# Exponentials in two runs of three, ternary magnitudes one iteration earlier, and GpSimd work in pieces, in a two-layer decoder on one NeuronCore

## What is computed

```python
x = x + L0_attn(ln(x))    # 16 heads of 16, RoPE, causal softmax, fp32 accuracy
x = x + L0_xattn(ln(x))   # fp8 quantised product with the context
x = x + L0_ffn(ln(x))     # mixture of 16 experts (top 4 of 2 groups) + shared expert
x = x + L1_attn(ln(x))    # ternary weights, int8 activations, causal softmax
x = x + L1_xattn(ln(x))   # 4 experts chosen by token id: silu(h W) * (h W), W^T
x = x + L1_ffn(ln(x))     # ternary gate/up/down with an inner RMS norm
```

## Time and profile before

| | |
|---|---|
| median of 3 runs | 726.19 us (725.18 to 727.3) |
| the profiled execution | 725.6 us, span 723.7 us |
| mean granted TensorE clock | 0.879 |
| PE busy | 527.7 us, 73% |
| DVE busy | 471.7 us, 65% |
| ACT busy | 343.7 us, 47% |
| POOL busy | 135.4 us, 19% |
| chain that ended last | PE 42%, DVE 32%, ACT 14%, issue 8% |

### The profile page before, as it was taken

The page is one execution under the profiler, slowest core; times in us unless marked ns, Lnnn a source line. Parts: engine busy times, 40 slices in busy tenths (PEclk is TensorE's granted clock), DMA queues, the critical chain, the costliest instruction groups (busy, mean ns, idle before and its releaser), DMA issues.

```text
span 723.7 us, 11688 instructions
## 1 busy us (share of the span) xinstructions
PE 527.7 (73%) x4689; PEld 362.9 (50%) x4716; DVE 471.7 (65%) x1049; ACT 343.7 (47%) x543; POOL 135.4 (19%) x142
## 2 busy tenths in 40 slices
PE   2663728527998789997789978999867677465775
PEld 1331414315676567675566756676645445233443
DVE  3667796796568864588645855458544664456985
ACT  2332416514772257822678226772478439213454
POOL 2225245350000400000040000004000040002543
PEclk9776768867999999999999999999989989769679
DMA  6032122201000010000000000001000000000000
GB/s 202 1 137 91 47 67 85 83 39 59 2 1 1 3 58 1 2 1 1 1 25 36 1 1 1 1 2 59 5 25 1 2 1 1 0 1 0 1 29 30
DMA packets 5706, 20.01 MB, mean 28 GB/s; under 512 B 879, under 2 KB 3055, under 8 KB 5012
## 3 DMA queue, kind: packets, MB, share of 16 engines
q1 hardware_dynamic: 5652, 19.26, 7.9%
HBM read 18.21 MB, written 1.05 MB: 27 GB/s over the span
## 4 chain that ended last, share of the span: by engine, by line
PE 42%; DVE 32%; ACT 14%; issue 8%; POOL 1%; DMA 1%; SPq 0%; ACTq 0%; DVEq 0%; POOLq 0%
PE ps L842 14%; PE ps L870 9%; ACT L1230 4%; DVE nmx L1555 4%; PE ps L627 4%; DVE hs L1670 3%; PE ps L737 2%; ACT hs L1230 2%; DVE hs L1664 2%; DVE y L1452 2%; PE ps L852 2%; PE ps L649 1%; PE ps L609 1%; DVE hl L1675 1%; ACT hh L1237 1%
## 5 line engine op out<-in xcount | busy, mean ns | idle before, releaser
L1237 ACT ACTIVATE hh<-hs 128x512 f16<-128x512 f32 (+1 forms) x68 | 42.0, 618 | 129.0 <-DVE hs L1670 129.0
L1664 DVE TENSOR_TENSOR hs<-hs,ps 128x512 f32<-128x512 f32 (+1 forms) x68 | 45.6, 670 | 81.0 <-ACT hs L1230 49.5
L487 POOL TENSOR_TENSOR ve<-mv,half 128x2 f32<-128x2 f32 x24 | 5.4, 224 | 344.7 <-DVE mv L1445 344.7
L1675 DVE TENSOR_TENSOR hl<-hs,hh 128x512 f16<-128x512 f32 (+1 forms) x68 | 49.3, 726 | 28.6 <-ACT hh L1237 28.0
L1555 DVE TENSOR_REDUCE nmx<-ps 128x2 f32<-128x512 f32 (+1 forms) x96 | 61.0, 680 | 3.8 <-PE ps L682 3.6
L870 PE MATMUL ps<-w2h,hh 128*128 128x256 f16 x200 | 55.8, 279 | 1.4 <-DVE hl L1675 1.3
L870 PE MATMUL ps<-w2l,hh 128*128 128x256 f16 x200 | 55.2, 276 | 0.0
L870 PE MATMUL ps<-w2h,hl 128*128 128x256 f16 x200 | 55.1, 276 | 0.0
L1230 ACT ACTIVATE hs<-ps 128x512 f32<-128x512 f32 (+1 forms) x68 | 39.6, 582 | 23.6 <-PE ps L842 23.2
L1670 DVE TENSOR_TENSOR hs<-hs,ps 128x512 f32<-128x512 f32 (+1 forms) x68 | 45.2, 665 | 1.1
L1230 ACT ACT_TABLE_LOAD x35 | 44.9, 1283 | 0.6
(11 more groups left out here) (245 smaller groups left out, 1352.3 us busy)
## 6 DMA issues: line engine op xcount, KB each, us to landing
stage<-in_w SPq DMA_DIRECT2D x12, 800.0 KB, 4.2
tstage<-in_tern SPq DMA_DIRECT2D x4, 1024.0 KB, 4.9
cs<-in_ctxT SPq DMA_DIRECT2D x1, 1024.0 KB, 10.1
out_x<-xs SPq DMA_DIRECT2D x4, 256.0 KB, 2.2
w0s<-in_w SPq DMA_DIRECT2D x1, 768.0 KB, 7.1
xs<-in_x SPq DMA_DIRECT2D x1, 768.0 KB, 8.4
lnwb<-in_lnw SPq DMA_DIRECT2D x1, 512.0 KB, 3.7
xs<-in_x SPq DMA_DIRECT2D x1, 256.0 KB, 2.7
```

Source lines behind the costliest of these rows:

```text
L1237: act.activation(hh[:, n % 2, 0:w], hs[:, n % 2, 0:w], ACT.Copy).then_inc(e_hi.sem, 1)
L1664: TT(hs[:, n % 2, 0:w], hs[:, n % 2, 0:w], ps[:, up_bank(n), 0:w], ALU.mult).then_inc(e_hb.sem, 1)
L1675: TT(hl[:, n % 2, 0:w], hs[:, n % 2, 0:w], hh[:, n % 2, 0:w], ALU.subtract).then_inc(e_lo.sem, 1)
```

## The change

Four edits:

1. In the mixed iterations ACT does E0, E1, E2 in a run, then the Silus of pairs 0 to 2, then E3, E4, E5 in a run, then the Silus of pairs 3 and on. PE's and DVE's lists are rewritten to match, also for iterations 0 and 1, which have no pairs. `phase_a` now holds pairs 0 to 5 and the second phase begins with pair 6.
2. `magnitudes(2)` and `magnitudes(3)` move from `phase_a` of iterations 5 and 6 to late in iterations 4 and 5.
3. POOL's `split_lo` becomes four instructions of 400 columns instead of one of 1600; its product with the norm weight in the last feed-forward becomes two of 256 instead of one of 512.
4. In iteration 0, `context_scaled` on DVE stands ahead of `queries_keys(1, 0)` and not behind it, and `context_rounded(2)` behind both `low_parts`.

```diff
+LOW_PIECE = 400
...
             def split_lo(b, n):
                 g.wait_ge(wst_hi.sem, wst_hi.at(b, n + 1))
-                g.tensor_tensor(wl[n][:, b * W_SLICE:(b + 1) * W_SLICE], stage[:, n, :],
-                                wh[n][:, b * W_SLICE:(b + 1) * W_SLICE], ALU.subtract).then_inc(wst_lo.sem, 1)
+                for a in range(0, W_SLICE, LOW_PIECE):
+                    cols = slice(b * W_SLICE + a, b * W_SLICE + a + LOW_PIECE)
+                    last = g.tensor_tensor(wl[n][:, cols], stage[:, n, a:a + LOW_PIECE], wh[n][:, cols], ALU.subtract)
+                last.then_inc(wst_lo.sem, 1)
...
-                    g.tensor_tensor(fw[:, j, c * 512:(c + 1) * 512], fh[:, j, c * 512:(c + 1) * 512],
-                                    lnwb[:, c * 512:(c + 1) * 512], ALU.mult).then_inc(f_w.sem, 1)
+                    for a in (512 * c, 512 * c + 256):
+                        last = g.tensor_tensor(fw[:, j, a:a + 256], fh[:, j, a:a + 256], lnwb[:, a:a + 256], ALU.mult)
+                    last.then_inc(f_w.sem, 1)
```

PE's `phase_a`, first half, before and after (`-` and `+`):

```diff
                 ups(it, 0)
                 scores_exp(it, 1)
-                outs(it, 0)
+                if it + 1 >= B:
+                    first_turn(it + 1)
+                scores_exp(it, 2)
                 if it + 1 < B:
                     project(it + 1, 0)
+                if routes:
+                    router_norm_turned(it - 1)
+                scores_exp(it, 3)
+                outs(it, 0)
                 gates(it, 1)
                 if it + 1 >= B:
-                    first_turn(it + 1)
-                if routes:
-                    router_norm_turned(it - 1)
+                    project(it + 1, 0)
                 ups(it, 1)
-                scores_exp(it, 2)
-                outs(it, 1)
-                if it + 1 >= B:
-                    project(it + 1, 0)
-                gates(it, 2)
                 if routes:
                     logits(it - 1)
                 values(it, 0)
+                outs(it, 1)
+                gates(it, 2)
+                values(it, 1)
                 ups(it, 2)
-                scores_exp(it, 3)
                 outs(it, 2)
-                values(it, 1)
+                back(it, 0)
+                project(it + 1, 1)
                 gates(it, 3)
                 ups(it, 3)
-                back(it, 0)
-                project(it + 1, 1)
                 scores_exp(it, 4)
-                outs(it, 3)
-                gates(it, 4)
                 scores_exp(it, 5)
-                ups(it, 4)
-                outs(it, 4)
                 values(it, 2)
-                gates(it, 5)
                 if it + 1 < ITS:
                     stack(it + 1, 0)
                     stack(it + 1, 1)
-                ups(it, 5)
+                outs(it, 3)
+                gates(it, 4)
```

DVE's `phase_a`, first part:

```diff
-                hb(it, 0)
                 if it + 1 < B:
                     first_low(it + 1)
                 elif it + 1 < ITS:
                     first_norm(it + 1)
                 if routes:
                     normalised("router", it - 1, yr, False)
-                hc(it, 0)
+                if it == 0:
+                    context_scaled()
                 if it + 1 < B:
                     queries_keys(it + 1, 0)
-                if it == 0:
-                    context_scaled()
-                low(it, 0)
-                hb(it, 1)
+                hb(it, 0)
                 if routes:
                     experts_lo("moe", it - 1, 0)
-                hc(it, 1)
+                hc(it, 0)
+                if it + 1 >= B:
+                    queries_keys(it + 1, 0)
+                low(it, 0)
```

ACT's `phase_b1`, where the magnitudes go:

```diff
+                sil(it, 9)
+                if it + 1 < ITS:
                     maxima_turned(it + 1)
+                experts_hi("hash", b, 7)
+                high(it, 9)
+                if b < 2:
+                    magnitudes(b + 2)
                 sil(it, 10)
```

More of the change, by code:

```diff
@@ L940, in phase_a, with phase_b0 @@
                     stack(it + 1, 3)
+                ups(it, 4)
+                values(it, 3)
+                outs(it, 4)
+                scores_max(it + 1, 0)
+                gates(it, 5)
+                back(it, 1)
+                ups(it, 5)
+                scores_max(it + 1, 1)
                 outs(it, 5)
-                values(it, 3)
-                scores_max(it + 1, 0)
+            def phase_b0(it):
                 gates(it, 6)
-                back(it, 1)
+                turn32(o, o_ok.sem, o_ok.at(it, 2))
                 ups(it, 6)
-                scores_max(it + 1, 1)
+                scores_max(it + 1, 2)
                 outs(it, 6)
[L950 to L956, removed]
                 pe.wait_ge(f_lo.sem, f_turn["output", it] + 1)
@@ L963, in phase_b0 @@
                 mm.then_inc(att_ok.sem, 1)
+                gates(it, 7)
+                scores_max(it + 1, 3)
+                ups(it, 7)
+                outs(it, 7)
                 gates(it, 8)
-                scores_max(it + 1, 3)
+                turn16(qq, q_ok, it + 1)
                 ups(it, 8)
+                scores_max(it + 1, 4)
                 outs(it, 8)
[L968 to L971, removed]
                 if it == 0:
@@ L979, in phase_b0 @@
                 mm.then_inc(xa_ok.sem, 1)
+                gates(it, 9)
+                scores_max(it + 1, 5)
+                ups(it, 9)
                 outs(it, 9)
-                scores_max(it + 1, 5)
                 if it:
@@ L998, in phase_b1 @@
                 b = it - B
-                gates(it, 7)
[L1000 to L1005, removed]
+                gates(it, 6)
+                scores_max(it + 1, 2)
+                ups(it, 6)
+                turn16(qq, q_ok, it + 1)
+                outs(it, 6)
+                scores_max(it + 1, 3)
+                gates(it, 7)
                 pe.wait_ge(q_ev.sem, q_turn["output", b] + 1)
@@ L1011, in phase_b1 @@
                 mm.then_inc(att_ok.sem, 1)
+                ups(it, 7)
+                scores_max(it + 1, 4)
+                outs(it, 7)
+                gates(it, 8)
+                scores_max(it + 1, 5)
                 ups(it, 8)
-                scores_max(it + 1, 4)
                 outs(it, 8)
[L1015 to L1018, removed]
                 if b == 0:
                     router_turned(it)
+                gates(it, 9)
                 if it + 1 < ITS:
                     maxima_turned(it + 1)
+                ups(it, 9)
+                turn32(yr, y_ok.sem, ln_turn["tail", b] + 1)
+                outs(it, 9)
                 gates(it, 10)
                 ups(it, 10)
-                turn32(yr, y_ok.sem, ln_turn["tail", b] + 1)
                 outs(it, 10)
@@ L1253, in phase_a @@
                 exponentials(it, 1)
-                high(it, 0)
                 if it + 1 >= B:
                     first_turn(it + 1)
+                exponentials(it, 2)
+                sil(it, 0)
                 if routes:
@@ L1269, in phase_a @@
                 exponentials(it, 3)
-                high(it, 2)
                 stacks(it + 1, 0)
@@ L1324, in phase_b1 @@
                 b = it - B
+                sil(it, 6)
+                quantised("output", b)
+                high(it, 6)
                 sil(it, 7)
-                quantised("output", b)
                 high(it, 7)
@@ L1329, in phase_b1 @@
                 high(it, 8)
-                sil(it, 9)
-                high(it, 9)
                 if b == 0:
@@ L1791, in phase_b0 @@
                 moments_of("context", b)
-                low(it, 7)
+                low(it, 6)
                 maximum(it + 1, 3)
+                hb(it, 7)
                 normalised("context", b)
@@ L1812, in phase_b0 @@
                 link(last)
+                hc(it, 8)
+                low(it, 8)
                 if b:
@@ L1829, in phase_b0 @@
                 dve.wait_ge(x_ok.sem, 2 * b + 2)
+                hb(it, 10)
                 hc(it, 10)
@@ L1836, in phase_b1 @@
                 int8(o, [(scal[:, :], 1)])
-                hb(it, 7)
+                hb(it, 6)
                 maximum(it + 1, 2)
-                hc(it, 7)
-                low(it, 7)
+                hc(it, 6)
+                low(it, 6)
                 maximum(it + 1, 3)
```

113 lines of the change are left out of this document (54 added, 59 removed).

## The result

The changed kernel takes 751.55 us (median of 4 runs, 749.01 to 755.99), the kernel before 726.75 us: ratio 1.0348, 95% interval 1.0299 to 1.0396, so it is slower. The profiled execution took 749.0 us, its span is 747.1 us.

What follows compares the result with a forecast made beforehand. PE paces the mixed iterations, DVE ends iteration 0. Mixed +12.9, iteration 6 -0.5, iteration 7 +4.0, iterations 0 and 1 -11, feed-forward -1.2 sum to +4.2 on 726.2: 730.4 us; own range 724 to 740, with most of the faster rival 713 to 740.

Steps and rivals of the forecast that it cites:

- the wait for `vt`: Iteration 5, sign of being right: PE waits 2 to 3.5 us for the copied values.
- the start of iteration 1: Sign of being right: iteration 1's first Exp starts at about 100 us instead of 109.
- Table loads: ACT, whole kernel: 46 loads fewer take 59 us off ACT; at most what PE or DVE waits for comes back.
- The walk: Iteration 5, new lists timed item by item with row durations: +4.3 us, PE's work unchanged; iteration 3 alike: +3.6.
- the slower rival: Slower, as forecast, chance 0.52; its clock case: five iterations each lose 1.5 us more behind new waits, 738 us.
- For iterations 2 and 4 I take +2.5: Mixed iterations 2 and 4: +2.5 us each, an old stall at the second phase's end being partly filled.
- Iterations 0 and 1: Early context_scaled and shorter waits for POOL's pieces: -9 and -2 us, sum -11, bounds -5 and -15.
- Iteration 6: Walk gives 66.2 after against 66.7 before: -0.5 us; magnitudes leave, but the Exp runs hold pairs 0 and 3 back.
- Iteration 7: No other work there; Silu 3 comes behind E5 and the int8 output is turned later: +4.0 us.
- Feed-forward: Last feed-forward: halves of POOL's product save about 0.4 us of `y` in each of three places: -1.2 us.
- the loads were the pace: Faster rival, chance 0.32: mixed iterations win 1 us each, 707 us, or 716 with half; needs copied-values wait under 1 us.
- The halves cancel: Rival, chance 0.16: mixed iterations lose 2 us each, iterations 0 and 1 win 11: 726 us.

Runs made afterwards that it cites:

- e7: Changed kernel, but iterations 2 to 7 keep the order of before up to pair 2, the new order from pair 3: 718.32 us, ratio 0.9891.
- e10: e9 with the lists of e7 in iteration 6 alone: 712.02 us, ratio 0.9783.
- e6: Changed kernel, but in iterations 2 to 7 all three engines return to the order of before from pair 3 on: 748.01 us, ratio 1.0265.
- e1: Changed kernel with the new lists in iterations 0 and 1 alone, lists of before in 2 to 7, POOL's pieces kept: 716.41 us, ratio 0.9837.
- e5: Changed kernel with ACT's copy of the values and stacks moved ahead of high 2, the load and Exp E3: 731.74 us, ratio 1.0046.
- e8: e3 plus, in mixed iterations, unneeded matmuls in PE's waits for the copied values and for qh: 738.87 us, ratio 1.0153.
- e3: Changed kernel with PE's wait for the copied values moved behind the queries' and keys' part of the projection: 746.41 us, ratio 1.0256.
- e11: e10 plus 8 unneeded matmuls in PE's wait for qh (iterations 3 to 6) and e3's edit: 715.94 us, ratio 0.9830.
- e4: e3 plus 2 or 5 unneeded repeats of a product while PE waits for the copied values: 749.84 us, ratio 1.0311.
- e2: Kernel before the change with only POOL's work in pieces: 720.04 us, ratio 0.9886.
- e9: e1 with magnitudes 2 and 3 moved behind high 10 of iterations 4 and 5: 715.38 us, ratio 0.9841.

## Why the prediction was wrong

It said 730.4 us and a range of 713 to 740; the time is 751.55, 24.8 us over the kernel before where 4.2 were forecast. The direction was the forecast's, the size was not. Of the signs it named, the wait for `vt`, the 24 loads, `ce` and the start of iteration 1 (100.5 us) came true; iteration 5 took 90.6 us and not 86 to 88.

- **Table loads** ("46 x 1.28 = 59 us leave ACT", little comes back): right. ACT's busy time fell by 58.8 us, from 343.7 to 284.9, and the kernel became slower. The rule of the Trainium skill to group activations by table set (ScalarE: Activation LUTs, "Rules for kernel authors") is not borne out where ACT is not what others wait for; e7 and e10 show it paying in iteration 6 alone.
- **The walk, as to places**: right. It named the wait for the copied values with 2.9 us, and 2.9 was measured; the waits for `qh` (1.8, measured 1.9), for the scores' banks (2.2, measured 2.8) and for the Silus behind E5 and behind the magnitudes (1.3 and 1.25, measured 1.0 and 1.1) are there too. "PE's waits go from about 9 to 14 us": PE's idle time went from 8.0 to 13.2.
- **The walk, as to size**: this is the step that failed. "The difference, +4.3 us, is what I use", with "its work is the same", was a walk at full clock. Measured was +7.6 in iteration 5 and +8.8 in iteration 3 (+3.6 predicted). PE's idle time grew by 5.2 and 4.3 us, near what the walk has. Its busy time, which the walk kept, grew by 2.4 and 4.4 us, while the low time went from 3.3 to 10.9 us in iteration 5 and from 7.2 to 17.8 in iteration 3. I had the clock only as a case within the slower rival, 1.5 us an iteration, and outside the sum; the trace has the clock at 0.50 right behind the new wait (476 to 479 us).
- **"For iterations 2 and 4 I take +2.5"**: not walked, and too small: +5.5 and +4.8. The clock adds about 1 us in iteration 2 (PE's busy time went from 83.0 to 84.1) and nothing in iteration 4 (0.98 both times). PE's idle time, length less busy, grew by 4.4 us in iteration 2 (10.5 to 14.9) and by 5.0 in iteration 4 (10.7 to 15.7), as much as in the iterations that I did walk. All four together: +26.6 against +12.9. Of the 13.7 missing, 7.7 are the same work done slower (PE's busy time) and 6.0 are waits, 4.4 of them in the two iterations that were not walked. Half of the low time (44 against 23 us) would give 10.4 for the clock; that is the upper estimate.
- **Iterations 0 and 1** (-9 and -2): -9.7 and -2.0. Right, and for the reason given: `ce` and `cm` came down to 1.85 us (predicted under 2.5), `prob` and `gt` from 1.93 and 3.04 to 0.65 and 0.35. By the rule of the Trainium skill on the shared port (SBUF - State Buffer, "SBUF: two separate sides") only what is left of a piece has to be waited for. The trace agrees: 1.85 us less the 1.1 of `ce`'s own work is 0.75, and a piece takes about 0.9. The -15 that the prediction drew from it was too much, since the waits were not all that made these iterations long.
- **Iteration 6** (-0.5): +1.4, the wrong sign; the first run loses, the second gains (75.0 us in e6 and 64.1 in e7, against 70.3 in e1). **Iteration 7** (+4.0): +5.7 with the last experts; the waits of PE there have 5.0 us for Exps against 0.6 before and 1.8 more for `hl`, against 2.4 less for `hs`. e6 has +6.2 there and e7 +4.5, so either run alone costs about as much as both.
- **Feed-forward** (-1.2): `y` in its three places went from 5.4 to 4.5 us, so 0.9 was saved, but the clock of this part was 0.77 instead of 0.83 and the part took 62.9 us instead of 62.5.
- **The rival "the loads were the pace"** (0.32): its condition was a wait for the copied values of under 1 us. That wait was 2.9 us, and without it (e5) the kernel is still not faster (ratio 1.0046). *The halves cancel* (0.16): iterations 0 and 1 won the 11 us, but the mixed ones lost 6.7 us each and not 2.

## What to carry to other kernels

Before grouping one engine's work to save its table loads, look who waits for that engine, and then for the small copies that now stand behind the group: here one of 0.46 us behind a load and two Exps was waited for in five iterations, 2.9 us each time, and moving it won 20 us. Price a new wait of a busy TensorE at more than its length, since the work behind it may run at half the clock; the number to compare is the time at the lower level, from the windows of both traces. And test an order by halves: one half of this one cost nothing in the sum, and the best kernel uses it in the one iteration where it pays.

## What the runs showed of the hardware

- Matmuls that nobody needs, put in waits of PE, made a kernel 7.5 us faster (e8 against e3) in an order with many waits. Another, in an order with few, got 4 us slower with them and with e3's edit (e11 against e10). In e4 the low stretches only moved.
- Pieces of 400 columns instead of 1600 on GpSimd cost it 0.44 us each time where VectorE is not in its way: nine of the twelve low parts took 3.2 us before, and eight of them about 3.65 in four pieces. Its busy time grew from 135.4 to 143.1 us. With the halves in the last feed-forward this gave 7.8 us to the kernel (e2), most of it by shorter waits of VectorE (4.5 us for `ce` and `cm`).
- The waiting goes both ways. In iteration 0 of the kernel before `w1l` took 4.91 us and not 3.2: it started at 54.42, VectorE's `cq` ended at 56.25, and 56.25 + 3.2 is 59.4, where it ended (59.33). `w3l` behind it took 4.18 us, about one `ce` of 1.1 longer than 3.2. So in this stretch the long instructions of the two engines went one after the other, each whole.
